# Last weight row spread by TensorE, and rewritten first steps, in the first layer of a two-layer kernel on Trainium2

## The chip, the cores and the metric

The kernel runs on one core of a Trainium2 chip. The metric is the device time of one execution in microseconds (us). TensorE is called PE here, its weight loads PEld, VectorE is DVE, ScalarE is ACT, GpSimd is POOL; SyncE (SP) issues most DMAs.

## What is computed

8192 rows of 256 go through two layers. This is the reference, cut to the first layer, the only one that the change touches:

```python
xn = _layernorm(x, axis=-1)
qkv = xn @ W;  q, k, v = jnp.split(qkv, 3, axis=-1)        # W: 256 x 768
q = elu(q) + 1;  k = elu(k) + 1
KV = einsum('bld,blh->bhd', k, v);  Z = 1 / (q . k.sum + EPS)
s = einsum('bld,bhd,bl->blh', q, KV, Z)                     # linear attention
g = silu(ffn(xn))      # the expert with the largest xn @ gate_w.T, of 8
x = x + s * g
```

The second layer has block attention, a gate with routed attention heads, and the same closing sum.

## The kernel before

All of the program is written out by hand, engine by engine; semaphores (named in `g`) tie the engines together, and what stands in an engine's function is the order in which that engine works. It has three stages: the first layer's attention with the sorting of rows by expert (to about 217 us), the experts, the second layer. The change lies in `first_layer`.

**Units and steps.** The 8192 rows are 32 units of 256 rows. Each engine has a function `step(n, i, r)` and runs it for n up to 31 in its own order. For a unit n the work goes: SP loads x into `four`; DVE takes means and variances (`norm_stats`, `find_moments`, `variance_eps`); POOL makes 1/sqrt and the shift (`norm_scale`, lines 895 and 897); ACT applies them and writes `xn` (`norm_apply`, line 529); PE transposes xn (`turn`, line 394); ACT rounds the transposed tile to fp32r and DVE takes the rest, so that a value is the sum of two fp32r numbers (`round_turned`, `split_turned`); PE makes q (`q`, 12 products of 256 columns) and k with the gate's logits (`keys`, 12 products of 264 columns); ACT takes the exponentials (`exp_q`, `exp_keys`), DVE completes them (`fill_q`, `fill_keys`), k is rounded and split (`round_keys`, `split_keys`), and PE adds k's products with xn to a sum (`sums`, 12 products). In PE's step n stand turn(n+1), q(n), keys(n) and sums(n-1). A product of two split matrices is three matmuls (`mm3`, lines 167 to 169). Every fourth unit closes a row of the batch, and `kv` multiplies the sum with the value weights; the first such product is in step 5.

**The trick with the last column.** `xn` has 1.0 in its last column in place of the last normalized value, and the last row of W is subtracted from every row of W ("centring"), since normalized rows sum to zero. The same last row is needed on all 128 partitions. Before, a DMA brings it there: `row_end`, a `partition_broadcast` of 3 KB to 128 partitions (384 KB), issued by SP behind the first part of W and ahead of the 8 KB gate weights and of the other parts. DVE's `centre_weights(part)` (lines 762 to 772) subtracts it from 256 columns of W (the parts are the weights of q, k and v) and, for q and k, adds the last column of the identity matrix to the last half, as

```python
m = nc.vector.tensor_tensor(cols, cols, row_end[...].to_broadcast([P, KD, D]), ALU.subtract)
m = nc.vector.tensor_scalar(cols[:, KD - 1, :], cols[:, KD - 1, :], z.ident[:, P - 1:P], None, ALU.add)
```

Then ACT rounds the weights (`round_weights`, line 603) and DVE takes the rest (`split_weights`, line 778): piece 0 is q's, 1 is k's, 2 is the gate's 16 columns, 3 is the values'. PE turns the gate weights with two tiny transposes (line 507) once DVE has centred them (`centre_gate`, line 760).

**The first steps.** The steps with n at most 0 differ: DVE centres parts 0 and 1 in step -2, splits pieces 0 to 2 and centres part 2 in step -1, and splits piece 3 at the start of step 1; ACT rounds pieces 0 to 2 in step -2 and piece 3 at the end of step 0.

## Time and profile before

| | |
|---|---|
| median of 3 runs | 536.98 us (535.69 to 537.85) |
| the profiled execution | 538.56 us, its span 536.9 us |
| PE busy | 503.0 us, 94% of the span |
| DVE, ACT, POOL busy | 458.7 us, 392.1 us, 315.3 us |

The span is the time between the first and the last instruction that the profiler saw. A busy PE counts matmuls whose ends are modelled, so the start-to-start distance of two matmuls says more than the duration of one. In a timeline row the bracket at the end gives how long the engine had been idle before the row, and whose work ended that.

### The profile page before, as it was taken

How to read it: one execution, taken by the hardware profiler on the slowest of the kernel's cores; microseconds unless marked ns; L12 is line 12 of the kernel's file. 1: busy time of each engine (PE TensorE's matmuls, PEld its weight loads, DVE VectorE, ACT ScalarE, POOL GpSimd, SP SyncE). 2: the span in 40 equal slices, each digit the busy share in tenths (PEclk: the TensorE clock that was granted, in tenths of full speed). 3: DMA queues.
4: the chain of work that ended last, by engine and by line, in shares of the span. 5: the costliest groups of instructions: out<-in, count | busy, mean ns of one | idle time of the engine just before them, and what ended most of it. 6: DMA issues, size and time to landing. Idle time of an engine off the chain costs nothing.

```text
span 536.9 us, 12508 instructions
## 1 busy us (share of the span) xinstructions
PE 503.0 (94%) x3554; PEld 464.4 (87%) x3555; DVE 458.7 (85%) x1475; ACT 392.1 (73%) x891; POOL 315.3 (59%) x395
## 2 busy tenths in 40 slices
PE   1899999999999999898999997899999999999995
PEld 0899999999999998787999985788888888888884
DVE  4698999999999887478787837899999999999985
ACT  3687878787878764476777744678887888779883
POOL 4458876667777876222222026868888888786410
PEclk9999999999999999899999999999999999999999
DMA  8933222222222115556677563235655656555311
GB/s 229 234 97 108 92 94 100 84 79 79 80 81 89 41 70 188 147 168 196 212 249 209 181 213 104 77 98 121 135 129 129 139 122 131 124 145 110 74 59 60
DMA packets 59552, 68.12 MB, mean 127 GB/s; under 512 B 11880, under 2 KB 53744, under 8 KB 59504
## 3 DMA queue, kind: packets, MB, share of 16 engines
q1 hardware_dynamic: 45104, 39.73, 24.4%
q0 software_dynamic: 14400, 27.80, 21.2%
q8 instruction: 24, 0.39, 0.3%
q14 instruction: 24, 0.20, 0.1%
HBM read 40.25 MB, written 27.26 MB: 126 GB/s over the span
## 4 chain that ended last, share of the span: by engine, by line
PE 59%; DVE 20%; issue 8%; POOL 6%; DMA 3%; ACT 3%; DVEq 1%; SPq 0%; POOLq 0%; ACTq 0%
PE gu_ps L1083 5%; PE v_ps L1483 4%; PE q_ps L1461 3%; PE t_ps L1059 3%; PE k_ps L167 3%; PE y_ps L1102 3%; DVE zg L1710 3%; PE k_ps L168 3%; PE tq_ps L167 3%; PE k_ps L169 3%; PE m_ps L167 3%; PE tq_ps L168 3%; PE m_ps L169 2%; PE tq_ps L169 2%; PE tq_ps L394 2%
## 5 line engine op out<-in xcount | busy, mean ns | idle before, releaser
L1830 POOL DMA_INDIRECT four<-expert_rows,gather_u x64 | 69.0, 1078 | 40.7 <-DMA expert_rows<-y 22.3
L914 POOL DMA_INDIRECT sorted_rows<-xn,row_u x64 | 68.0, 1063 | 17.2 <-issue 13.9
L903 POOL TENSOR_TENSOR xn<-xn 128x512 fp32r<-128x512 f32 x32 | 43.3, 1353 | 32.1 <-ACT xn L539 31.9
L1461 PE MATMUL q_ps<-xt,wqk 128*128 128x256 f32 x256 | 61.4, 383 | 0.8 <-ACT xt L1579 0.8
L1483 PE MATMUL v_ps<-wvo,xt 128*128 128x256 f32 x256 | 60.5, 379 | 0.0
L1461 PEld LDWEIGHTS q_ps<-xt,wqk 128*128 128x128 f32 x256 | 49.2, 193 | 7.8 <-ACT xt L1579 1.0
L205 POOL DMA_DIRECT2D four<-sorted_rows x36 | 19.4, 539 | 62.3 <-issue 32.2
L1848 POOL TENSOR_TENSOR rstd<-var_eps,neg_half 128x4 f32<-128x4 f32 x32 | 38.5, 1204 | 20.7 <-DVE var_eps L1704 11.0
L1483 PEld LDWEIGHTS v_ps<-wvo,xt 128*128 128x128 f32 x256 | 46.3, 190 | 5.0
L1599 ACT ACTIVATE xn2nd<-res,shift,rstd 128x256 f32<-128x256 f32 (+1 forms) x64 | 34.9, 594 | 19.3 <-POOL shift L1850 19.2
L1083 PE MATMUL gu_ps<-wgu,xgt 128*128 x288 | 40.2, 283 | 0.0
L529 ACT ACTIVATE xn<-four,shift,rstd 128x255 f32<-128x255 f32 x64 | 34.9, 601 | 5.9 <-POOL shift L897 5.9
L167 PE MATMUL tq_ps<-xt,wq 128*128 128x256 f32 x128 | 39.0, 305 | 0.0
L567 ACT ACTIVATE k<-kf 128x512 fp32r<-128x512 f32 x32 | 20.2, 630 | 25.0 <-DVE kf L681 25.0
L167 PE MATMUL k_ps<-wkg,xt 128*128 128x264 f32 x128 | 38.0, 297 | 0.0
L167 PE MATMUL m_ps<-k,xn 128*128 128x256 f32 x128 | 36.3, 284 | 1.2 <-DVE k L687 1.2
L168 PE MATMUL k_ps<-wkg,xt 128*128 128x264 f32 x128 | 36.8, 287 | 0.0
L169 PE MATMUL k_ps<-wkg,xt 128*128 128x264 f32 x128 | 36.6, 286 | 0.0
L1083 PEld LDWEIGHTS gu_ps<-wgu,xgt 128*128 128x128 f32 x288 | 35.0, 191 | 1.5
L168 PE MATMUL tq_ps<-xt,wq 128*128 128x256 f32 x128 | 36.3, 283 | 0.0
L169 PE MATMUL tq_ps<-xt,wq 128*128 128x256 f32 x128 | 36.2, 283 | 0.0
L169 PE MATMUL m_ps<-k,xn 128*128 128x256 f32 x128 | 36.1, 282 | 0.0
(253 smaller groups left out, 1774.2 us busy)
## 6 DMA issues: line engine op xcount, KB each, us to landing
expert_rows<-y SPq DMA_DIRECT2D x36, 256.0 KB, 2.8
four<-in_L_attn_x SPq DMA_DIRECT2D x32, 256.0 KB, 2.9
out_rows<-att SPq DMA_DIRECT2D x32, 256.0 KB, 2.5
res<-in_L_attn_x POOLq DMA_DIRECT2D x24, 256.0 KB, 4.4
four<-sorted_rows SPq DMA_DIRECT2D x36, 128.0 KB, 2.2
four<-sorted_rows POOLq DMA_DIRECT2D x36, 128.0 KB, 2.6
wdn<-in_L_ffn_wd SPq DMA_DIRECT2D x2, 512.0 KB, 7.2
sorted_rows<-res SPq DMA_DIRECT2D x8, 128.0 KB, 6.1
```

The source lines that it names most:

```text
L167: nc.tensor.matmul(out, lhs[0], rhs[0], start=first, stop=False, **kw)
L168: nc.tensor.matmul(out, lhs[0], rhs[1], start=False, stop=False, **kw)
L169: return nc.tensor.matmul(out, lhs[1], rhs[0], start=False, stop=last, **kw)
L529: m = nc.scalar.activation(xn[:, i, t, 0:D - 1], xa[:, i % X_SLOTS, t, 0:D - 1], ACT.Identity, bias=shift[:, i % X_SLOTS, t:t + 1], scale= ...
L903: nc.gpsimd.tensor_tensor(xn2[:, s, 1], xn[:, i], xn2[:, s, 0].bitcast(F32), ALU.subtract).then_inc(g["xn_split"], 1)
L914: nc.gpsimd.indirect_dma_start(out=z.sorted_dram.ap(), out_offset=bass.IndirectOffsetOnAxis(ap=row_u[:, i // CU, k:k + 1], axis=0), in_=xn ...
L1083: m = nc.tensor.matmul(gu_ps[:, i % 2, u * 2 * DE:(u + 1) * 2 * DE], xgt[:, i, k, u, :], z.wgu[:, k, bass.ds(e[u], 1), :].rearrange("p a f ...
L1461: m = nc.tensor.matmul(q_ps[:, j, :], wqk[:, k, j * P:(j + 1) * P], xt[:, i % 2, k, :], start=(j == 0 and k == 0), stop=(k == KD - 1), ski ...
L1483: m = nc.tensor.matmul(v_ps[:, t, :], xt[:, i % 2, k, t * P:(t + 1) * P], wvo[:, k, :], start=(t == 0 and k == 0), stop=(k == KD - 1), ski ...
L1599: m = nc.scalar.activation(xn[:, i % SLOTS, t, :].unsqueeze(1), one_tile(n, t), ACT.Identity, bias=shift[:, i % SLOTS, t:t + 1], scale=rst ...
L1830: nc.gpsimd.indirect_dma_start(out=moe[:, i % SLOTS, t, :], out_offset=None, in_=z.expert_dram.ap(), in_offset=bass.IndirectOffsetOnAxis(a ...
L1848: nc.gpsimd.tensor_tensor(rstd[:, i % SLOTS], var_eps[:, i % SLOTS], z.neg_half[:, 0:2 * UT].rearrange("p (a t) -> p a t", a=2), ALU.pow). ...
```

## The change

1. The broadcast DMA of the last row goes. In its place PE multiplies a 128x128 selector matrix (`last_row`, whose row 127 is all ones, made by one DVE copy of the identity's last column) with the last half of each part of W (`spread_end`): this puts the last row on all 128 partitions of a PSUM bank (`row_ends`). `centre_weights` reads it from there.
2. PE makes eight products of the identity with itself that nobody reads (`stay_warm`): six at the very start, two in step 0.
3. PE's step 0 has q(0) ahead of turn(1), and PE starts when the identity alone is there instead of all constants.
4. DVE: the split of q's weights comes right behind the centring in step -2, that of k's and the gate's behind the first split of xt in step -1, the centring of the value weights in step 0 together with `fill_q(0)` ahead of the rest, and the split of the value weights at the end of step 2.
5. ACT: in step -2 only q's weights are rounded; those of k and of the gate follow the first transposed tile; exp_q(0) comes ahead of the normalization of unit 2; the value weights are rounded ahead of `round_keys(0)`.
6. POOL makes its five casts (line 927) one step earlier, ahead of the scale of unit 1.
7. The wait and the copy of the selector stand in DVE's part a second time, at the end of the layer ahead of `table_rows`.

```diff
@@ -266,7 +266,7 @@
-        row_end = z.res[:, 4 * UT:4 * UT + 3].rearrange("p t d -> p (t d)")
+        last_row = kf[:, 1].rearrange("p t d -> p (t d)")[:, 0:P]
@@ -274,7 +274,7 @@
-        g = sems("gate_loaded moe_w_loaded ends_loaded blank consts cast gate_centred gate_turned part_centred centred rounded split step "
+        g = sems("gate_loaded moe_w_loaded selector ends_spread blank consts cast gate_centred gate_turned part_centred centred rounded split step "
@@ -321,6 +321,8 @@
         values_before = lambda n: sum(s < n for s in BESIDE_STEPS)
 
         gate_ps = v_ps[:, 0, 0:KD * E].rearrange("p (k e) -> p k e", e=E)
+        row_ends = (m_ps[:, 0, 0:D], m_ps[:, 1, 0:D], v_ps[:, 1, 0:D])
+
 
         kv_bank = lambda b: m_ps if b == UNITS // ROW - 1 else v_ps
 
@@ -352,7 +354,6 @@
                     cols = slice(part * D, (part + 1) * D)
                     sp.dma_start(w_s[:, :, cols], W[:, cols].rearrange("(k p) n -> p k n", p=P)).then_inc(w_loaded[part], 16)
                     if part == 0:
-                        sp.dma_start(row_end, W[D - 1, :].partition_broadcast(P)).then_inc(g["ends_loaded"], 16)
                         sp.dma_start(gate_s[:], gate_w).then_inc(g["gate_loaded"], 16)
 
             def step(n, i, r):
@@ -488,12 +489,26 @@
                                     [kv2[:, ORDER[p] // ROW - SPLIT_ROWS[0], a, j, :] for a in range(2)], j == 0, j == KD - 1)
                     m.then_inc(z.v_ready, 1)
 
+            def spread_end(part):
+
+                pe.wait_ge(w_loaded[part], 16)
+                nc.tensor.matmul(row_ends[part], last_row, w_s[:, KD - 1, part * D:(part + 1) * D], start=True, stop=True).then_inc(g["ends_spread"], 1)
+
+            def stay_warm(count):
+                for _ in range(count):
+                    nc.tensor.matmul(k_ps[:, 0, 0:P], z.ident[:], z.ident[:], start=True, stop=True)
+
             def step(n, i, r):
+                begin = n == 0
+                if begin:
+                    stay_warm(2)
+                    spread_end(2)
+                    pe.wait_ge(g["split"], 1)
+                    q(n, i, r)
                 turn(n + 1, at(i, 1))
-                if isinstance(n, int) and n == 0:
-                    pe.wait_ge(g["split"], 1)
-                q(n, i, r)
-                if isinstance(n, int) and n == 0:
+                if not begin:
+                    q(n, i, r)
+                if begin:
                     pe.wait_ge(g["split"], 3)
                     pe.wait_ge(g["cast"], 5)
                 keys(n, i, r)
@@ -501,11 +516,15 @@
                 sums(n - 1, at(i, -1), r if i else r - 1)
                 values(n)
 
-            pe.wait_ge(g["consts"], 6)
+            pe.wait_ge(g["consts"], 1)
+            stay_warm(6)
+            pe.wait_ge(g["selector"], 1)
+            spread_end(0)
             pe.wait_ge(g["gate_centred"], 1)
             for k in range(KD):
                 t = nc.tensor.transpose(gate_ps[:, k], gate_c[:, k * P:(k + 1) * P], z.ident[0:E, 0:E])
             t.then_inc(g["gate_turned"], 1)
+            spread_end(1)
             run(pe, -1, step, UNITS - 1)
             whole_values(nc, pe, z, TAIL[0], tail_banks(TAIL[0]), SPLIT)
             count(UNITS, 0, 0)
@@ -608,21 +627,26 @@
                 round_sums(n, i, r)
                 if begin and n == -2:
                     norm_apply(0, 0)
-                    round_weights((0, 1, 2))
+                    round_weights((0,))
                 round_turned(n + 1, at(i, 1))
+                if begin:
+                    exp_q(n, i)
+                if begin and n == -1:
+                    round_weights((1, 2))
                 if begin and n > -2:
                     norm_apply(n + 2, at(i, 2))
                 round_xn(n, i)
                 rows(value_of(n - 1))
-                exp_q(n, i)
+                if not begin:
+                    exp_q(n, i)
                 if not begin:
                     norm_apply(n + 2, at(i, 2))
                 exp_keys(n, i)
                 round_kv(n, i, r)
                 round_next(value_of(n + 1))
-                round_keys(n, i)
                 if begin and n == 0:
                     round_weights((3,))
+                round_keys(n, i)
 
             run(act, -2, step, UNITS - 1)
             rows(TAIL[0])
@@ -761,12 +785,10 @@
 
             def centre_weights(part):
                 cols = w_s[:, :, part * D:(part + 1) * D]
-                dve.wait_ge(w_loaded[part], 16)
-                dve.wait_ge(g["ends_loaded"], 16)
-                m = nc.vector.tensor_tensor(cols, cols, row_end[:, part * D:(part + 1) * D].unsqueeze(1).to_broadcast([P, KD, D]), ALU.subtract)
+                dve.wait_ge(g["ends_spread"], part + 1)
+                m = nc.vector.tensor_tensor(cols, cols, row_ends[part].unsqueeze(1).to_broadcast([P, KD, D]), ALU.subtract)
                 if part < 2:
                     m.then_inc(g["part_centred"], 1)
-                    dve.wait_ge(g["consts"], 6)
                     dve.wait_ge(g["part_centred"], part + 1)
                     m = nc.vector.tensor_scalar(cols[:, KD - 1, :], cols[:, KD - 1, :], z.ident[:, P - 1:P], None, ALU.add)
                 m.then_inc(g["centred"], 1)
@@ -846,33 +868,39 @@
                     centre_gate()
                     centre_weights(0)
                     centre_weights(1)
-                if begin and n == -1:
-                    split_weights((0, 1, 2))
+                    split_weights((0,))
+                if begin and n == 0:
                     centre_weights(2)
-                if begin and n == 1:
-                    sum_columns()
-                    split_weights((3,))
+                    fill_q(n, i)
                 split_keys(n - 1, at(i, -1))
                 split_kv(n - 1)
                 divisors(value_of(n - 1))
                 if there(n):
                     split_sums(n, i, r)
                 split_turned(n + 1, at(i, 1))
+                if begin and n == -1:
+                    split_weights((1, 2))
                 split_next(value_of(n))
                 norm_stats(*ahead)
                 stats_complete(*ahead)
-                fill_q(n, i)
+                if not (begin and n == 0):
+                    fill_q(n, i)
                 find_moments(*ahead)
                 negate_mean(*ahead)
                 variance_eps(*ahead)
                 fill_keys(n, i)
                 route_and_place(n, i, r)
                 keep_pick(n, i, r)
+                if n == 2:
+                    sum_columns()
+                    split_weights((3,))
                 if isinstance(n, int) and n >= UNITS - 8 and n % CU == 0:
                     centre_experts((n - UNITS + 8) // CU)
 
             nc.vector.memset(one_col[:], 1.0)
             nc.vector.memset(change[:, E - 1:E], 0.0)
+            dve.wait_ge(g["consts"], 1)
+            nc.vector.tensor_copy(last_row, z.ident[:, P - 1:P].to_broadcast([P, P])).then_inc(g["selector"], 1)
             run(dve, -3, step, UNITS - 1)
             split_keys(UNITS - 1, SLOTS - 1)
             divisors(TAIL[0])
@@ -882,6 +910,8 @@
             table_owners()
             table_offsets()
             divisors(TAIL[1])
+            dve.wait_ge(g["consts"], 1)
+            nc.vector.tensor_copy(last_row, z.ident[:, P - 1:P].to_broadcast([P, P])).then_inc(g["selector"], 1)
             table_rows()
             divisors(TAIL[2])
             table_names()
@@ -921,7 +951,7 @@
 
             def step(n, i, r):
                 norm_scale(n + 2, at(i, 2))
-                if isinstance(n, int) and n == -1:
+                if isinstance(n, int) and n == -2:
                     for dst, src in ((z.ones_b, ones_s), (z.before, tri_s), (z.causal, causal_s),
                                      (z.ident_b, z.ident[:]), (z.slot_id, ids[:])):
                         nc.gpsimd.tensor_copy(dst[:], src).then_inc(g["cast"], 1)
```

PE's first instructions before (`tq_ps` holds the transposed tile and q, `v_ps<-ident,gate_c` are the gate's transposes):

```order
L507 MATMUL v_ps<-ident,gate_c 128x8 [waits first_gate_centred,first_consts]
L507 MATMUL v_ps<-ident,gate_c 128x8
L394 MATMUL tq_ps<-ident,xn 128x128 [waits first_xn_ready]
L394 MATMUL tq_ps<-ident,xn 128x128 x3
L394 MATMUL tq_ps<-ident,xn 128x128 [waits first_t_split,first_xn_ready]
L394 MATMUL tq_ps<-ident,xn 128x128 x3
L167 MATMUL tq_ps<-xt,wq 128x256 [waits first_t_split,first_split]
```

and after the change (`k_ps<-ident` are the unread products, `<-w_s,kf` the spreading of the last row):

```order
L499 MATMUL k_ps<-ident 128x128 [waits first_consts]
L499 MATMUL k_ps<-ident 128x128 x5
L495 MATMUL m_ps<-w_s,kf 128x256 [waits w_loaded0,first_selector]
L525 MATMUL v_ps<-ident,gate_c 128x8 [waits first_gate_centred]
L525 MATMUL v_ps<-ident,gate_c 128x8
L495 MATMUL m_ps<-w_s,kf 128x256 [waits w_loaded1]
L395 MATMUL tq_ps<-ident,xn 128x128 [waits first_xn_ready]
L395 MATMUL tq_ps<-ident,xn 128x128 x3
L499 MATMUL k_ps<-ident 128x128 x2
L495 MATMUL v_ps<-w_s,kf 128x256 [waits w_loaded2]
L167 MATMUL tq_ps<-xt,wq 128x256 [waits first_t_split,first_split]
```

Eight unread products and three spreading products are new, and q(0), the row with `tq_ps<-xt,wq`, now stands ahead of the second group of transposes.

DVE from the end of the centring to the value weights' centring, before (`w_s` is W, `wq` and `wkg` the split weights, `xt` the transposed tile):

```order
L640 BN_STATS stats<-four 128x6 [waits x_loaded1]
L640 BN_STATS stats<-four 128x6
L652 BN_AGGR moments<-stats 128x2 [waits first_stats_done]
L652 BN_AGGR moments<-stats 128x2
L658 TENSOR_SCALAR neg_mean<-moments 128x2 [waits first_moments_ready]
L663 TENSOR_SCALAR var_eps<-moments 128x2
L778 TENSOR_TENSOR wq<-w_s,wq 128x512 [waits first_rounded]
L778 TENSOR_TENSOR wkg<-w_s,wkg 128x2x256 [waits first_rounded]
L778 TENSOR_TENSOR wkg<-v_ps,wkg 128x2x8 [waits first_rounded]
L766 TENSOR_TENSOR w_s<-w_s,res 128x2x256 [waits first_ends_loaded,w_loaded2]
L668 TENSOR_TENSOR xt<-tq_ps,xt 128x512 [waits first_t_rounded]
```

and after:

```order
L800 TENSOR_TENSOR wq<-w_s,wq 128x512 [waits first_rounded]
L664 BN_STATS stats<-four 128x6 [waits x_loaded1]
L664 BN_STATS stats<-four 128x6
L676 BN_AGGR moments<-stats 128x2 [waits first_stats_done]
L676 BN_AGGR moments<-stats 128x2
L682 TENSOR_SCALAR neg_mean<-moments 128x2 [waits first_moments_ready]
L687 TENSOR_SCALAR var_eps<-moments 128x2
L692 TENSOR_TENSOR xt<-tq_ps,xt 128x512 [waits first_t_rounded]
L800 TENSOR_TENSOR wkg<-w_s,wkg 128x2x256 [waits first_rounded]
L800 TENSOR_TENSOR wkg<-v_ps,wkg 128x2x8 [waits first_rounded]
```

The split of `wq` has moved ahead of the statistics of unit 1, the first split of `xt` stands right behind them, and the splits of `wkg` and the centring of the value weights come later.

ACT behind its first normalization, before (`kf` and `k` belong to the keys, `res` to q):

```order
L603 ACTIVATE wq<-w_s 128x512 [waits first_centred]
L603 ACTIVATE wkg<-w_s 128x2x256 [waits first_centred]
L603 ACTIVATE wkg<-v_ps 128x2x8 [waits first_gate_turned]
L544 ACTIVATE xt<-tq_ps 128x512 [waits first_t_ready]
L529 ACTIVATE xn<-four,shift,rstd 128x255 [waits first_shift_ready]
L529 ACTIVATE xn<-four,shift,rstd 128x255
L544 ACTIVATE xt<-tq_ps 128x512 [waits first_t_ready]
L529 ACTIVATE xn<-four,shift,rstd 128x255 [waits first_shift_ready]
L529 ACTIVATE xn<-four,shift,rstd 128x255
L539 ACTIVATE xn<-xn 128x512 [waits first_xn_ready]
L552 ACTIVATE res<-tq_ps,minus_one 128x512 [waits first_q_ready]
L560 ACTIVATE kf<-k_ps,minus_one 128x512 [waits first_k_ready]
```

and after:

```order
L622 ACTIVATE wq<-w_s 128x512 [waits first_centred]
L563 ACTIVATE xt<-tq_ps 128x512 [waits first_t_ready]
L622 ACTIVATE wkg<-w_s 128x2x256 [waits first_centred]
L622 ACTIVATE wkg<-v_ps 128x2x8 [waits first_gate_turned]
L548 ACTIVATE xn<-four,shift,rstd 128x255 [waits first_shift_ready]
L548 ACTIVATE xn<-four,shift,rstd 128x255
L563 ACTIVATE xt<-tq_ps 128x512 [waits first_t_ready]
L571 ACTIVATE res<-tq_ps,minus_one 128x512 [waits first_q_ready]
L548 ACTIVATE xn<-four,shift,rstd 128x255 [waits first_shift_ready]
L548 ACTIVATE xn<-four,shift,rstd 128x255
L558 ACTIVATE xn<-xn 128x512 [waits first_xn_ready]
L579 ACTIVATE kf<-k_ps,minus_one 128x512 [waits first_k_ready]
```

The first `xt` is one copy earlier, `res` (exp_q(0)) is ahead of unit 2's normalization, and the last row is k's exponential in both.

## Rows read from the trace of the kernel before

**Rows 1.** The page, busy time of each engine: us, share of the span, instructions.

```profile
PE 503.0 (94%) x3554; PEld 464.4 (87%) x3555; DVE 458.7 (85%) x1475; ACT 392.1 (73%) x891; POOL 315.3 (59%) x395
```

**Rows 2.** Windows: stretch, length, busy of PE, PEld, DVE, ACT, POOL, PEclk, DMA.

```profile
40.00:60.00 20.00, 20.00 (x177) 19.90 (x177) 18.09 (x69) 16.14 (x30) 17.68 (x21) 1.00 0.33 107
...
180.00:200.00 20.00, 20.00 (x178) 19.90 (x177) 17.30 (x60) 14.59 (x29) 15.81 (x16) 1.00 0.16 61
```

**Rows 3.** Timeline of PE: start, duration, engine, line, operation, count, idle before.

```profile
14.63 1.11 PE L394 MATMUL tq_ps<-ident,xn 128*128 128x128 f32 x4 [4.91 <-ACT xn L529]
...
15.76 0.41 PE L168 MATMUL tq_ps<-xt,wq 128*128 128x256 f32 x1
...
18.10 0.42 PE L167 MATMUL k_ps<-wkg,xt 128*128 128x264 f32 x1
...
19.64 0.36 PE L168 MATMUL k_ps<-wkg,xt 128*128 128x264 f32 x1
...
20.32 0.60 PE L394 MATMUL tq_ps<-ident,xn 128*128 128x128 f32 x4
...
24.60 0.36 PE L167 MATMUL m_ps<-k,xn 128*128 128x256 f32 x1 [0.80 <-DVE k L687]
...
26.11 0.60 PE L394 MATMUL tq_ps<-ident,xn 128*128 128x128 f32 x4
```

**Rows 4.** Windows of PE alone: stretch, length, busy, granted clock, DMA share, GB/s.

```profile
15.74:19.80 4.06, 4.06 (x21) 1.00 1.11 210
```

**Rows 5.** Timeline of SP, issues of the first two weight parts.

```profile
1.44 0.46 SPq L353 DMA_DIRECT2D w_s<-in_L_attn_W  x1
...
2.88 0.39 SPq L353 DMA_DIRECT2D w_s<-in_L_attn_W  x1
```

**Rows 6.** DMA issues in 1.4 to 1.9 and in 2.85 to 3.3: us to landing.

```profile
w_s<-in_L_attn_W SPq DMA_DIRECT2D x1, 256.0 KB, 2.9
w_s<-in_L_attn_W SPq DMA_DIRECT2D x1, 256.0 KB, 5.8
```

**Rows 7.** Timeline of DVE in the first 25 us.

```profile
7.84 0.34 DVE L760 TENSOR_SCALAR gate_c<-gate_s 8x256 f32<-8x256 f32 x1 [2.83 <-DMA gate_s<-in_L_ffn_gate_w]
8.11 0.67 DVE L766 TENSOR_TENSOR w_s<-w_s,res 128x512 f32<-128x512 f32 x1
...
10.22 0.74 DVE L640 BATCH_NORM_STATS2 stats<-four 128x6 f32<-128x256 f32 x2
...
11.36 0.16 DVE L663 TENSOR_SCALAR var_eps<-moments 128x2 f32<-128x2 f32 x1
...
13.32 0.68 DVE L668 TENSOR_TENSOR xt<-tq_ps,xt 128x512 fp32r<-128x512 f32 x1
...
23.16 0.69 DVE L778 TENSOR_TENSOR wv<-w_s,wv 128x512 fp32r<-128x512 f32 x1 [0.92 <-ACT wv L603]
23.76 0.69 DVE L687 TENSOR_TENSOR k<-kf,k 128x512 fp32r<-128x512 f32 x1
```

**Rows 8.** Timeline of ACT in the first 23 us.

```profile
6.20 1.09 ACT L529 ACTIVATE xn<-four,shift,rstd 128x255 f32<-128x255 f32 x2 [3.97 <-POOL shift L897]
...
15.78 0.60 ACT L544 ACTIVATE xt<-tq_ps 128x512 fp32r<-128x512 f32 x1 [1.20 <-PE tq_ps L394]
...
20.53 0.69 ACT L560 ACTIVATE kf<-k_ps,minus_one 128x512 f32<-128x512 f32 x1 [1.50 <-PE k_ps L169]
21.97 0.63 ACT L567 ACTIVATE k<-kf 128x512 fp32r<-128x512 f32 x1 [0.75 <-DVE kf L681]
```

**Rows 9.** Timeline of POOL, two of its reciprocal square roots.

```profile
11.60 1.07 POOL L895 TENSOR_TENSOR rstd<-var_eps,neg_half 128x2 f32<-128x2 f32 x1 [5.44 <-DVE var_eps L663]
...
15.30 0.71 POOL L895 TENSOR_TENSOR rstd<-var_eps,neg_half 128x2 f32<-128x2 f32 x1 [0.72 <-DVE var_eps L663]
```

**Rows 10.** Timelines of DVE and of SP at the end of the layer.

```profile
214.56 0.20 DVE L835 CAST row_i<-first_row 128x72 int32<-128x72 f32 x1
...
216.81 5.47 SPq L205 DMA_DIRECT2D four<-sorted_rows  x5
```

## The prediction, made before the changed kernel ran

> **What bounds the kernel now.** I read the page first: PE is busy for 94% of the span [rows 1]. The windows then show where it is not. From 40 to 60 us and from 180 to 200 us PE is busy for all 20.00 us while DVE has 1.9 to 2.7 us left [rows 2]; the six windows of 20 us between these two also have PE at 20.00. So once the layer runs, PE is the bound, its work is fixed, and whatever the start saves is kept. The timeline of PE shows the start: it waits 4.91 us until 14.63, when unit 1 is normalized, waits another 0.80 us at 24.60 for DVE's split of k, and reaches turn(3) at 26.11 [rows 3]. Behind that it has no idle time worth a row until 200 us. **The time of turn(3) is therefore the quantity to predict.** Before, it is 26.11.
>
> PE also runs at half rate at first. The granted clock reads 1.00 from 15.74 to 19.80 [rows 4], but the 11 products from 15.76 to 18.10 are (18.10 - 15.76)/11 = 0.213 us apart, which is 256 columns at 1.2 GHz; at 19.64 the durations begin to fall from 0.42, and the 12 products from 24.60 to 26.11 are 0.126 us apart, the 2.4 GHz level [rows 3]. PE had worked without a pause from 14.63 before it rose.
>
> **Where the start waits.** The first part of W is issued at 1.44 and lands 2.9 us later, at 4.34; the second is issued at 2.88 and needs 5.8, to 8.68 [rows 5, 6]. Between them in the queue stand only the broadcast of 384 KB and the gate's 8 KB. DVE is idle for 2.83 us until the gate weights land at 7.84, and from there it works without a gap: centring from 8.11, statistics of unit 1 from 10.22 to 11.52, first split of xt at 13.32 [rows 7]. POOL and ACT add 1.07 us and more, and that makes the 14.63 of PE [rows 3, 9].
>
> **The change, part by part.**
>
> *Loads.* Without the broadcast the gate and the second part are issued one place earlier, near 2.0 and 2.4. Bounds for the second part's landing: 2.4 + 2.9 = 5.3 if it takes what the first did, 2.4 + 5.8 = 8.2 if the broadcast was not what delayed it. I take 5.3, since the first part had no broadcast ahead of it and is the nearest row.
>
> *Selector and unread products.* The DVE copy of 128x128 falls into DVE's idle time ahead of 3.7 us, before x has come: 0. If that cover were gone it would cost at most the 0.69 us of a 512-wide operation [rows 7]. The six unread products run between about 2 and 4.6 us, when PE has nothing else. An fp32 product of 256 columns at half rate has no row here. Its bounds are the 0.41 us that a rounded one lasts and twice that, 0.82 [rows 3]; I take the upper one for it, because it must not be late: 4.34 + 0.82 = 5.2.
>
> *Centring.* DVE is free at 7.84 - 2.83 = 5.01. The gate takes 8.11 - 7.84 = 0.27, so part 0 is centred from about 5.4, by which time its spread row is there, and part 1 follows; both took 10.22 - 8.11 = 2.11 [rows 7], so 7.5. The operand is now in PSUM: the split of xt, which reads PSUM, takes 0.68 us, the centring out of SBUF 0.67 [rows 7], so I add nothing. The Trainium skill (VectorE: DVE Perf Modes, the TRN2 errata) speaks against this edit, since it gives an operation on PSUM a fixed cost of 120 cycles instead of 58; that would be about 0.07 us each, 0.14 us for the two centrings on the path; the rows do not show it.
>
> *Up to q(0).* ACT normalizes unit 0 from 6.20 for 1.09 us [rows 8], then rounds q's weights until 7.9. DVE splits them (0.60 to the next start, 23.76 - 23.16) until 8.5, does the statistics of unit 1 (1.2, from 10.22 to just behind the start at 11.36) until 9.7 and splits xt until 10.4 [rows 7]. PE turns unit 0 at 7.4, ACT has it rounded by 7.4 + 1.15 + 0.60 = 9.2 [rows 3, 8], so it is not late. q(0) starts at 10.4.
>
> *PE's first block.* turn(1), q(0) and keys(0) took 20.32 - 14.63 = 5.69 at mostly half rate [rows 3]. In the new order and at the same rate they end at 16.1, turn(1) starting at 10.4 + 12 x 0.213 = 13.0. It needs unit 1: its variance is ready at 9.8, and from POOL's start at 11.60 to PE's at 14.63, over POOL and ACT, 3.0 us passed [rows 3, 9], so 12.8. It is 0.2 in time. The two fillers and the spreading of part 2 stand in the wait ahead of 10.4.
>
> *ACT.* Its copy of unit 1's tile follows 15.78 - 14.63 = 1.15 after the turn [rows 3, 8], at 14.15. Behind it stand that copy, exp_q(0), two normalizations and one rounding, about 0.55 + 0.55 + 1.0 + 0.55 = 2.65 by the starts of such rows, so k's exponential begins at 16.8, not at 20.53 [rows 8]: 3.7 earlier.
>
> *From there to turn(3).* Before, 20.53 to 21.97 (exponential, completion), then the rounding, DVE's split of the value weights at 23.16 and only then that of k at 23.76, sums(0) at 24.60 [rows 3, 7, 8]. After, DVE comes to k's completion about 0.3 late, since fill_q(0), the split of xt and the statistics stand ahead; rounding at 16.8 + 1.44 + 0.3 = 18.5, split of k over by 19.9, for the 0.60 of the value weights no longer stands there. PE meanwhile does turn(2) and q(1), waits to 18.6 for keys(1), and ends it at 20.1; sums(0) takes 26.11 - 24.60 = 1.5, to 21.6 [rows 3]. Unit 3 is normalized at 21.7. **turn(3) stands at 21.8, so the gain is 26.11 - 21.8 = 4.3 us.**
>
> *What is late next.* The split of the value weights and sum_columns are put at the end of step 2, 0.60 + 0.25 on DVE. The step before it carried the routing, this one does not, and kv comes only in step 5: 0. The gate's and k's splits behind xt are done by 11.5, keys(0) asks at 13.8: 0. POOL's casts run beside DVE's centring: 0. At the layer's end the second copy of the selector costs DVE up to 0.7, but the table is written at 214.56 + 0.20 and SP issues the loads that need it at 216.81 [rows 10]: 0, with 2.0 us of cover.
>
> **Sum.** The profiled execution took 538.56 us, so it becomes 534.3. That execution lay 1.6 above the median of 536.98, and against the median I predict 536.98 - 4.3 = **532.7 us**. The three runs lie 2.2 apart, so about 0.5% (2.7 us) is what a measurement can tell from no change.
>
> **Rivals.**
>
> *Full rate earlier (0.25).* PE now works from 7.4 to about 9.4 and again from 10.4, instead of pausing for 4.91 us. If that lets the clock rise by 13.0, then turn(1) and keys(0) take half, some 1.6 us less, of which ACT's chain lets through 0.7: gain 5.0, 532.0 us. For it: PE's pause of 4.91 us ahead of the half-rate stretch [rows 3]. Against it: PE rose only after 5 us of unbroken work then. The Trainium skill (TensorE: Matmul & The Clock Gate, Part 1 and Part 4) says that activity releases the throttle at a moment that varies from run to run, and that transposes do not count as activity as products do; by that the unread products would bring this case about, and no row here separates the two.
>
> *The lag moves to DVE (0.10).* DVE has 1.9 us left in 20 [rows 2] and is 0.3 later against PE than before. If every early step then costs PE 0.5 for four steps, the gain is 2.3: 534.7 us. Against it: sums(1) still comes after the routing in my schedule.
>
> *The broadcast was not the delay (0.10).* If the gate still lands near 7.8, then centring starts as before and only the order helps: q(0) follows its own chain, 2.4 us later than above. Gain 1.9: 535.1 us. For it: landing times of 5.8 us at full queues [rows 6]. Against it: nothing else stood between the two landings.
>
> *Slower (0.05).* The half rate outlasts the new pauses. PE now stops near 13.0, 16.1 and 18.6, and if the clock only rises after unbroken work as from 14.63, it stays at 1.2 GHz, and each full step of 36 products costs 36 x (0.213 - 0.126) = 3.1 us more than at 2.4. It decides from 1.4 such steps on, where the 4.3 is used up; with 2.5 steps more at half rate the result is +3.5 us, 540.5.
>
> **How the numbers follow.** Forecast 0.50, the rivals 0.25, 0.10, 0.10 and 0.05. Faster by over 0.5% is the forecast and the first rival, 0.75; within 0.5% are the next two, 0.20; slower 0.05. The range starts at the first rival's 532.0 less 1.6 for the scatter of medians and a clock that rises earlier still, 530.4, and ends at the third rival's 535.1 plus 0.7 of scatter, 535.8; the slower case and the outer edges are left out. The forecast's own range is 531.2 to 534.2.
>
> **What would show it.** Gate weights centred near 5.0 instead of 7.84; q's first product near 10.4 and ahead of turn(1); k's exponential near 16.8; no wait of sums(0) for the value weights; turn(3) near 21.8; PE full from there; distances of 0.213 us until about 16. I am wrong if DVE still waits until 7.8 for a load, if turn(3) is early but PE shows idle time between 22 and 60 us, or if distances of 0.21 us go on behind 20 us.

## The result and the profile after

The changed kernel took **534.06 us** (median of 20 runs, 532.03 to 537.18), the one before 536.62 in the same comparison (20 runs). Two of those 20, at 577.24 and 642.45 us, stand far apart and are not in the ratio; the other 18 have a median of 536.26. The ratio is **0.9954, with an interval of 0.9938 to 0.9970**: faster by 2.5 us, between 1.6 and 3.3. The forecast was 532.7 us, from a gain of 4.3. The time lies in the range, and the gain is 1.8 us short: by its middle, 0.46%, it is just within the 0.5% that had been given 0.20, and not in the class above it that had 0.75; the interval reaches to 0.62%.

The profiled execution took 533.15 us, with a span of 531.5, against 538.56 and 536.9 before. That pair alone would say 5.4 us. Why the pair says 5.4 and the medians 2.5 is one of the two questions of this part; the other is which piece of the change made the gain. A part of the first is in the windows of the kernel before, columns as in [rows 2]:

```profile
218.00:224.00 6.00, 4.14 (x17) 3.16 (x16) 2.26 (x6) 2.88 (x6) 2.64 (x6) 0.77 0.70 221
```

The granted clock is 0.77 there and 1.00 in the same stretch of the changed kernel, and 6.0 x 0.23 = 1.4 us is an estimate of what that cost. With the 3.9 us of the start, below, it makes up 5.3 of the 5.4. The 1.4 belongs to this one execution and not to the change: a second profile of the kernel before reads 1.00 there. PE's work barely grew, by the rows of the eight unread products and the three that spread the row, two rows each [rows 1]:

```profile
PE 504.9 (95%) x3576; PEld 463.8 (87%) x3577; DVE 460.0 (87%) x1477; ACT 391.6 (74%) x891; POOL 315.7 (59%) x395
```

The windows of the changed kernel, columns as in [rows 2]. From 20 us on PE is busy for all of each stretch of 20 us, as far as 200:

```profile
12.00:15.00 3.00, 3.00 (x16) 3.00 (x15) 1.31 (x6) 1.49 (x4) 0.89 (x2) 0.50 1.27 223
20.00:40.00 20.00, 20.00 (x174) 19.55 (x173) 18.84 (x69) 15.96 (x31) 12.49 (x13) 1.00 0.50 158
180.00:200.00 20.00, 20.00 (x177) 19.90 (x176) 15.73 (x48) 14.35 (x27) 16.17 (x16) 1.00 0.17 66
```

The first row is of another kind. The granted clock reads 0.50 there, so PE was at 1.2 GHz from 12 to 15 us, *after* it had been at 2.4. The timeline of PE shows the same, and answers to [rows 3]:

```profile
4.73 0.73 PE L495 MATMUL m_ps<-w_s,kf 128*128 128x256 f32 x2
...
6.67 0.70 PE L495 MATMUL m_ps<-w_s,kf 128*128 128x256 f32 x2 [0.93 <-DMA w_s<-in_L_attn_W]
...
11.04 0.35 PE L167 MATMUL tq_ps<-xt,wq 128*128 128x256 f32 x1 [2.03 <-DVE xt L692]
...
11.35 0.28 PE L169 MATMUL tq_ps<-xt,wq 128*128 128x256 f32 x1
11.46 0.28 PE L167 MATMUL tq_ps<-xt,wq 128*128 128x256 f32 x1
...
12.02 0.41 PE L168 MATMUL tq_ps<-xt,wq 128*128 128x256 f32 x1
12.24 0.41 PE L169 MATMUL tq_ps<-xt,wq 128*128 128x256 f32 x1
...
13.09 1.05 PE L395 MATMUL tq_ps<-ident,xn 128*128 128x128 f32 x4
...
16.82 0.63 PE L395 MATMUL tq_ps<-ident,xn 128*128 128x128 f32 x4 [0.68 <-DVE xt L692]
...
19.04 0.39 PE L167 MATMUL k_ps<-wkg,xt 128*128 128x264 f32 x1 [0.18 <-DVE logit L706]
...
20.60 0.28 PE L167 MATMUL m_ps<-k,xn 128*128 128x256 f32 x1
...
22.18 0.65 PE L395 MATMUL tq_ps<-ident,xn 128*128 128x128 f32 x4
```

q(0) starts at 11.04 and its products are 0.12 us apart up to 11.82, then 0.21 apart until 15.04. turn(1) comes behind q(0), at 13.09, with no wait. keys(0) ends just before 16, turn(2) waits 0.68 us for DVE's split of xt, keys(1) waits 0.18, and sums(0) does not wait at all, where it waited 0.80 before [rows 3]. **turn(3) stands at 22.18 instead of 26.11: 3.93 us earlier.** The span less the time of turn(3) is 510.8 us before and 509.3 after, so in this pair the gain at the start is kept to the end.

DVE, answering to [rows 7]:

```profile
5.06 0.33 DVE L784 TENSOR_SCALAR gate_c<-gate_s 8x256 f32<-8x256 f32 x1
5.49 0.69 DVE L789 TENSOR_TENSOR w_s<-w_s,m_ps 128x512 f32<-128x512 f32 x1
...
7.40 0.69 DVE L789 TENSOR_TENSOR w_s<-w_s,m_ps 128x512 f32<-128x512 f32 x1 [0.73 <-PE m_ps L495]
...
8.40 0.68 DVE L800 TENSOR_TENSOR wq<-w_s,wq 128x512 fp32r<-128x512 f32 x1
...
15.39 0.69 DVE L699 SCALAR_TENSOR_TENSOR res<-res,tq_ps 128x512 f32<-128x512 f32 x1 [2.01 <-ACT res L571]
...
17.65 0.59 DVE L682 TENSOR_SCALAR neg_mean<-moments 128x2 f32<-128x2 f32 x1
...
18.22 0.68 DVE L705 SCALAR_TENSOR_TENSOR kf<-kf,k_ps 128x512 f32<-128x512 f32 x1
...
19.59 0.69 DVE L711 TENSOR_TENSOR k<-kf,k 128x512 fp32r<-128x512 f32 x1 [0.61 <-ACT k L586]
...
28.64 0.69 DVE L800 TENSOR_TENSOR wv<-w_s,wv 128x512 fp32r<-128x512 f32 x1
```

The gate weights are centred at 5.06 without a wait, where DVE had been idle for 2.83 us until 7.84. At 7.40 stands the one wait of DVE ahead of q(0) that the forecast did not have, 0.73 us for the spread row of part 1, which itself waited 0.93 us for that part (PE, 6.67). The load of part 1 and its us to landing, answering to [rows 5, 6]:

```profile
2.40 0.38 SPq L355 DMA_DIRECT2D w_s<-in_L_attn_W  x1
```

```profile
w_s<-in_L_attn_W SPq DMA_DIRECT2D x1, 256.0 KB, 4.2
```

And ACT, answering to [rows 8]:

```profile
16.75 0.68 ACT L579 ACTIVATE kf<-k_ps,minus_one 128x512 f32<-128x512 f32 x1
...
18.93 0.63 ACT L586 ACTIVATE k<-kf 128x512 fp32r<-128x512 f32 x1 [0.98 <-DVE kf L705]
```

### The profile page after: what moved, and what is told of

Read it like the earlier page. It is cut to its first block, busy times and chain, and to the rows that moved or that the text cites. A ratio compares the mean times of both kernels' runs of the same rounds, so it can differ in the third digit from the quotient of the medians.

```text
span 531.5 us, 12547 instructions
## 1 busy us (share of the span) xinstructions
PE 504.9 (95%) x3576; PEld 463.8 (87%) x3577; DVE 460.0 (87%) x1477; ACT 391.6 (74%) x891; POOL 315.7 (59%) x395
## 3 DMA queue, kind: packets, MB, share of 16 engines
q1 hardware_dynamic: 44960, 39.34, 24.3%
## 4 chain that ended last, share of the span: by engine, by line
PE 61%; DVE 21%; issue 7%; DMA 4%; POOL 3%; ACT 2%; DVEq 1%; SPq 1%; POOLq 0%; ACTq 0%
PE gu_ps L1113 5%; PE v_ps L1513 4%; PE q_ps L1491 3%; PE k_ps L167 3%; PE m_ps L167 3%; PE m_ps L169 3%; PE t_ps L1089 3%; PE m_ps L168 3%; PE tq_ps L167 3%; PE k_ps L168 3%; PE k_ps L169 3%; PE y_ps L1132 3%; PE tq_ps L168 3%; PE tq_ps L169 3%; DVE zg L1740 3%
## 5 line engine op out<-in xcount | busy, mean ns | idle before, releaser
L167 PE MATMUL tq_ps<-xt,wq 128*128 128x256 f32 x128 | 38.6, 302 | 2.0 <-DVE xt L692 2.0
L167 PE MATMUL m_ps<-k,xn 128*128 128x256 f32 x128 | 36.2, 283 | 0.4 <-DVE k L711 0.4
L169 PE MATMUL m_ps<-k,xn 128*128 128x256 f32 x128 | 36.1, 282 | 0.0
L168 PE MATMUL m_ps<-k,xn 128*128 128x256 f32 x128 | 36.1, 282 | 0.0
L168 PE MATMUL tq_ps<-xt,wq 128*128 128x256 f32 x128 | 36.0, 281 | 0.0
```

Of the source, the lines that this page charges most:

```text
L167: nc.tensor.matmul(out, lhs[0], rhs[0], start=first, stop=False, **kw)
L168: nc.tensor.matmul(out, lhs[0], rhs[1], start=False, stop=False, **kw)
L169: return nc.tensor.matmul(out, lhs[1], rhs[0], start=False, stop=last, **kw)
```

## The experiments

"Changed kernel again" and "kernel before again" are the same two programs on other chips. Within one comparison the kernels ran on one chip; the ratios are to the kernel before there. A kernel with one execution only, its profiled one, has no ratio.

| kernel | ratio to before | turn(3) in its profile |
|---|---|---|
| kernel before again | none | 25.56 |
| only the spread row | 0.9977 (0.9954 to 1.0001) | 24.71 |
| only the order | 1.0001 (0.9974 to 1.0027) | 24.34 |
| changed, no unread products | 0.9965 (0.9943 to 0.9987) | 23.22 |
| changed kernel again | 0.9953 (0.9930 to 0.9975) | 21.52 |
| changed, more unread products | 0.9933 (0.9910 to 0.9957) | 22.43 |
| changed, part 1 by ACT's queue | 0.9961 (0.9940 to 0.9982) | 21.53 |
| changed, value split early | none | 22.74 |
| changed, turn(1) ahead of q(0) | 0.9974 (0.9950 to 0.9997) | 24.30 |
| changed, keys sooner | 0.9948 (0.9926 to 0.9971) | 21.49 |
| keys sooner, waits filled | 0.9901 (0.9871 to 0.9932) | 21.57 |
| changed, wait at the layer's end filled | 0.9947 (0.9926 to 0.9969) | 21.06 |

**The kernel before, again.** No edit.

> The kernel before, looked at a second time. My theory: the two profiled executions lie 5.4 us apart in span and only 3.9 apart at turn(3), and the rest is TensorE's clock, which stands at half rate in other stretches in each execution. Then this look shows turn(3) within 1.5 us of 26.11, but not at it, with the distances of 0.213 us ending at another time than 19.8, and the eight transposes at the layer's end (1.71 us before) may take another time. The rival, that turn(3) does not depend on the clock's phase: 26.1 within 0.2 again.

Measured: 537.26 us, span 535.6. The timeline of PE:

```profile
14.81 1.11 PE L394 MATMUL tq_ps<-ident,xn 128*128 128x128 f32 x4 [4.91 <-ACT xn L529]
...
24.05 0.36 PE L167 MATMUL m_ps<-k,xn 128*128 128x256 f32 x1 [0.80 <-DVE k L687]
...
25.56 0.60 PE L394 MATMUL tq_ps<-ident,xn 128*128 128x128 f32 x4
```

The same program starts its first block 0.18 us later than in [rows 3] and is at turn(3) 0.55 us sooner, because the spacing fell from 0.21 to 0.12 us at 18.3 instead of 19.8. So turn(3) of one profiled execution is good to some 0.5 us, by the moment at which the clock rises.

**Only the spread row.** The loads without the broadcast, the selector and the products that spread the row, in the order of before:

```diff
-                        sp.dma_start(row_end, W[D - 1, :].partition_broadcast(P)).then_inc(g["ends_loaded"], 16)
+                nc.tensor.matmul(row_ends[part], last_row, w_s[:, KD - 1, part * D:(part + 1) * D], start=True, stop=True).then_inc(g["ends_spread"], 1)
```

> Only the broadcast is replaced by the spreading products; all orders stay as before, and there are no unread products. If the loads were what mattered, most of the gain is here: centring of part 0 near 5.6 instead of 8.11, turn(1) near 12.5, turn(3) near 24.2, ratio about 0.9965. If the order of the steps is what mattered, turn(3) stays at 25.5 or later and the ratio above 0.998.

```profile
13.15 1.10 PE L394 MATMUL tq_ps<-ident,xn 128*128 128x128 f32 x4 [3.31 <-ACT xn L539]
...
23.20 0.36 PE L167 MATMUL m_ps<-k,xn 128*128 128x256 f32 x1 [0.80 <-DVE k L697]
```

Unit 1 is normalized 1.5 us sooner (13.15 for 14.63), but the block of turn(1), q(0) and keys(0) still takes 5.78 us at half rate, and the wait of 0.80 us for k is still there. The loads did what was expected of them (part 0 centred at 5.84 for 5.6, turn(1) at 13.15 for 12.5), and turn(3), at 24.71, and the ratio of 0.9977 lie between the two cases; the interval of the ratio holds both 0.9965 and no gain.

**Only the order.** The broadcast stays; the steps, the splits and the unread products are those of the changed kernel:

```diff
-                turn(n + 1, at(i, 1))
+                begin = n == 0
+                if begin:
+                    stay_warm(2)
...
+                    q(n, i, r)
+                turn(n + 1, at(i, 1))
```

> The changed kernel with the broadcast DMA back in its old place and no spreading products; the new order of the steps and the unread products stay. If the loads mattered: gate weights land at 7.8 again, q(0) starts near 13.3, turn(3) near 24.3 (1.8 us gained by the order alone, as the third rival of the prediction had it), ratio about 0.997. If the two parts only work together, turn(3) stays near 26.

```profile
12.55 0.55 PE L167 MATMUL tq_ps<-xt,wq 128*128 128x256 f32 x1 [2.20 <-DVE xt L684]
...
15.25 1.05 PE L396 MATMUL tq_ps<-ident,xn 128*128 128x128 f32 x4
```

q(0) starts 2.1 us before PE's first turn of the kernel before, turn(3) is 1.2 to 1.8 us sooner than in its two profiles, as was expected (24.34 for 24.3), and yet the ratio is 1.0001 where 0.997 was: what turn(3) gained did not come out in the median, and why stays open. By their middles neither half gives the whole, 0.23% and 0.00% against 0.46%, but the interval of the first, 0.9954 to 1.0001, reaches to the ratio of the changed kernel, and that was measured on another chip. turn(3) is clearer: 0.9 to 1.4 us sooner by the spread row, 1.2 to 1.8 by the order, 3.4 to 4.6 by both. (Seven of the 12 executions of this kernel had a low mean clock; the section on the clock has more.)

**Turn(1) ahead of q(0).** The changed kernel with this one pair in its old order:

```diff
-                    pe.wait_ge(g["split"], 1)
-                    q(n, i, r)
                 turn(n + 1, at(i, 1))
-                if not begin:
-                    q(n, i, r)
+                if begin:
+                    pe.wait_ge(g["split"], 1)
+                q(n, i, r)
```

> Undoes one part of the changed kernel: in TensorE's step 0 the turn of xn(1) stands ahead of q(0) again. Theory (the lag is set by VectorE's and ScalarE's work on the tiles, and a turn that waits for xn(1) holds q(0) back by some 1 us): q(0) begins after turn(1), near 13.2 instead of 11.0 to 11.2, keys(0) near 14.0 as in the changed kernel or up to 0.6 later, and turn(3) between 21.8 and 22.6, where the changed kernel showed 22.18 and 21.52. Ratio to the kernel before 0.995 to 0.997. Rival (the order on TensorE is what the change gains by): turn(3) over 23.0 and a ratio of 0.998 or more.

```profile
13.07 1.12 PE L395 MATMUL tq_ps<-ident,xn 128*128 128x128 f32 x4 [2.79 <-ACT xn L547]
...
18.94 0.63 PE L395 MATMUL tq_ps<-ident,xn 128*128 128x128 f32 x4 [0.17 <-DVE xt L691]
```

The theory gave too little for this piece. turn(3), at 24.30, lies beyond the 23.0 that the rival asked for; the ratio of 0.9974 lies between the theory's 0.997 and the rival's 0.998, where "only the spread row" stands. The first row shows the mechanism: PE waits 2.79 us for ACT's xn(1), and turn(1), q(0) and keys(0) fill 5.87 us after it, nearly all at half rate (the spacing fell only at 17.9). In the changed kernel the same block begins at 11.04 and fills 5.78 to turn(2). So **moving q(0) into the wait for unit 1 is worth 2.1 us at turn(2)** in this pair of profiles. Some of that is the clock: against "no unread products", which has the new order and q(0) at half rate as well, it is 1.1 us (turn(2) at 17.88), with q(0) there 0.6 us late for its weights. The move needs the spread row, since without that q(0) has its operands 1.5 us later.

**No unread products.** Both calls of `stay_warm` go.

> The changed kernel without its eight unread products. They raised the clock before q(0) (distances of 0.12 us from 11.04 to 11.8), but it fell back before turn(1). My theory: without them q(0) runs at half rate throughout and ends at 13.3 instead of 13.1, and keys(0) may stay at half rate longer; turn(3) 22.2 to 22.8, ratio to the kernel before 0.995 to 0.997, that is no more than 0.5 us worse than the changed kernel. The rival, that the unread products carry the gain: turn(3) later than 23.5 and a ratio of 0.998 or more.

```profile
6.74 1.22 PE L495 MATMUL m_ps<-w_s,kf 128*128 128x256 f32 x2 [0.61 <-DMA w_s<-in_L_attn_W]
```

Measured 0.9965, where the theory had it, beside 0.9954 and 0.9953 with them: the intervals overlap, so time tells nothing apart. The profile does. The pair of rows that spreads part 1's row lasts 1.22 us here, 0.70 in the changed kernel (PE, 6.67), q(0) starts at 11.63 and runs at half rate until 15.15, and turn(3) is at 23.22, 1.0 to 1.7 us later than in the two profiles of the changed kernel: later than the theory's 22.2 to 22.8 and sooner than the rival's 23.5. Some 0.6 us of it stands ahead of q(0), where part 1's row comes later and DVE waits 1.06 us for it.

All profiles together: **with six unread products at 2.0 us, q(0) started at full rate in 8 of 10 profiles** (not in "only the order" and "turn(1) ahead of q(0)"), and in 5 of the 9 that spread the row by products, the pair of part 1 already lasted 0.70. **Without them, q(0) ran at half rate in all 4** (both profiles of before, "only the spread row", this one). Only this last one differs from the changed kernel in nothing else, so the count leans on one profile. What the early rise gives is partly taken back: in 3 of those 5 PE fell back to half rate during the first block, as in the changed kernel at 11.82.

**More unread products.** Three groups of two more between PE's early turns, gated so that they fall into the wait ahead of q(0):

```diff
+                    pe.wait_ge(g["rounded"], 1)
+                    stay_warm(2)
+                    pe.wait_ge(g["rounded"], 3)
+                    stay_warm(2)
+                    pe.wait_ge(g["stats_done"], 2 * UT)
+                    stay_warm(2)
```

> The changed kernel with eight more unread products in TensorE's wait ahead of q(0), in four pairs, each behind an event of that wait, the last behind the statistics of unit 1. They fill the 2.03 us between 9.0 and 11.04. My theory, that idle time ahead of q(0) let the clock fall back: products 0.12 us apart from q(0) through keys(0), turn(1) at 12.7 when unit 1 is normalized instead of 13.09, turn(3) at 21.4 to 21.6, 0.6 to 0.8 earlier than in the changed kernel. The rival, that TensorE's rate in step 0 is hidden behind ScalarE: turn(3) at 22.0 or later. The last pair may delay q(0) by up to 0.3 at half rate.

```profile
7.13 1.22 PE L495 MATMUL m_ps<-w_s,kf 128*128 128x256 f32 x2 [1.02 <-DMA w_s<-in_L_attn_W]
```

Two things at once. In this execution PE was still at half rate before 10.7 (the spread pair of part 1 lasts 1.22 us instead of 0.70), and part 1 landed 0.5 us later, so q(0) began at 12.30. From there PE was at full rate, and turn(3) followed 10.13 us behind q(0), against 11.14 in the first profile of the changed kernel and 10.37 in the second. turn(3) itself, at 22.43, missed the theory's 21.4 to 21.6 and lies where the rival had it, but by the late landing of part 1 and not because PE's rate is hidden. Ratio 0.9933: the middle is 0.2% better than the changed kernel's, the interval does not part them.

**The changed kernel again.** No edit.

> The changed kernel itself, looked at again, with the others of this call as neighbours. The clock rose early and fell back at 11.8 in its first look. If that is the chance of one execution, the half-rate stretch lies elsewhere now and turn(3) is between 21.6 and 22.8; the ratio to the kernel before is 0.995 within 0.002.

```profile
11.15 0.36 PE L167 MATMUL tq_ps<-xt,wq 128*128 128x256 f32 x1 [0.91 <-DVE xt L692]
...
16.18 0.63 PE L395 MATMUL tq_ps<-ident,xn 128*128 128x128 f32 x4 [1.19 <-DVE xt L692]
...
21.52 0.66 PE L395 MATMUL tq_ps<-ident,xn 128*128 128x128 f32 x4
```

Here the clock rose later, during the wait ahead of q(0) (the pair of part 1 at 6.26 still lasted 1.22 us), and held: the spacing is 0.12 us from 11.15 on. q(0) and turn(1) are over sooner, turn(2) therefore *waits longer* for DVE, 1.19 us for 0.68, and of the 1.6 us that the half rate had cost PE (half of 11.82 to 15.04) only 0.66 show at turn(3). Part 1 landed sooner here too, 3.8 us after its issue for 4.2; over the profiles without the broadcast it took from 3.8 to 4.7.

**Part 1 of the weights by ACT's queue.**

```diff
-                    load_weights((0, 1) if m == 0 else (2,))
+                    load_weights((0,) if m == 0 else (2,))
...
+            act.dma_start(w_s[:, :, D:2 * D], W[:, D:2 * D].rearrange("(k p) n -> p k n", p=P)).then_inc(w_loaded[1], 16)
```

> The changed kernel with the second part of W issued by ScalarE's DMA queue at its very start instead of third but one on SyncE's. In the changed kernel it landed at 6.6 and DVE waited 0.73 us for its spread row at 7.40. If the place in the queue is the delay, it lands by 5.3, the wait goes, q(0) starts at 10.3 and turn(3) 0.6 to 0.7 earlier, at 21.5. If the memory's rate is the delay, the first part or x land later by as much and turn(3) stays within 0.2 of 22.2.

```profile
w_s<-in_L_attn_W ACTq DMA_DIRECT2D x1, 256.0 KB, 3.6
w_s<-in_L_attn_W SPq DMA_DIRECT2D x1, 256.0 KB, 3.8
```

```profile
4.33 0.75 DVE L665 BATCH_NORM_STATS2 stats<-four 128x6 f32<-128x256 f32 x2 [2.03 <-DMA four<-in_L_attn_x]
...
6.54 0.69 DVE L790 TENSOR_TENSOR w_s<-w_s,m_ps 128x512 f32<-128x512 f32 x1 [0.67 <-PE m_ps L495]
```

Part 1 is issued 1.45 us sooner and lands at 0.95 + 3.6 = 4.55 instead of 6.6. But part 0 now takes 3.8 us instead of 3.0, and the first tile's statistics start at 4.33 instead of 3.85. DVE waits 0.67 us for part 0's row instead of 0.73 for part 1's, and q(0) starts at 11.17. **What one load gains the others lose**: in this profile another queue made no gain ahead of q(0), so the place in the queue was not the delay. turn(3) at 21.53 is what the first theory had named, but by luck: PE was at full rate from q(0) on, as in the second profile of the changed kernel, whose turn(3) stands at 21.52.

**The value weights split early**, where they stood before:

```diff
+                if begin and n == 1:
+                    sum_columns()
+                    split_weights((3,))
```

> The changed kernel with the rounding of the value weights behind that of k, and their split at the start of step 1, as before the change. DVE then waits for ScalarE and splits them ahead of k: 0.60 and the three small operations, 0.8 to 1.4 us before k's split. turn(3) 23.0 to 23.6. The rival, that ScalarE's normalization of unit 3 sets turn(3) anyway: 22.4 or earlier.

```profile
21.23 0.36 PE L167 MATMUL m_ps<-k,xn 128*128 128x256 f32 x1 [0.80 <-DVE k L711]
```

The wait of 0.80 us for k is back, to the hundredth what it was in [rows 3]. turn(3) is at 22.74, though q(0) began at 11.01, between the theory's 23.0 and the rival's 22.4. The new place is worth 0.6 us at turn(3) against the first profile of the changed kernel, in which the clock fell back as it did here, and costs nothing at step 2, where PE has no idle row.

**Keys sooner.** An attempt at a better kernel. DVE's step 0 takes the centring of part 2, the split of xt(1) and the keys' bias ahead of the next moments, ACT takes k's exponential ahead of the rounding of xn(0) and rounds the value weights a step later, and the selector is not copied again:

```diff
+                    split_turned(n + 1, at(i, 1))
...
+                    norm_stats(*ahead)
+                    stats_complete(*ahead)
+                    fill_keys(n, i)
...
+                if begin:
+                    exp_keys(n, i)
```

> Adds to the changed kernel: VectorE's step 0 takes the centring of part 2, the split of xt(1), the keys' bias and only then the moments of the next tiles, ScalarE takes the keys' exponential of step 0 ahead of the rounding of xn(0), the value weights are rounded a step later, and the second copy of the selector goes. Theory (after the first projection the lag is the work on VectorE and ScalarE in order, not TensorE): turn(2) near 15.8 and turn(3) at 20.5 to 20.9, against 16.18 and 21.52, and a ratio near 0.9935. Rival (by then TensorE at its granted clock or the keys' chain elsewhere sets the lag): turn(3) at 21.3 or later and a ratio of 0.995 as in the changed kernel.

```profile
10.96 0.36 PE L167 MATMUL tq_ps<-xt,wq 128*128 128x256 f32 x1 [1.92 <-DVE xt L694]
...
12.64 1.11 PE L395 MATMUL tq_ps<-ident,xn 128*128 128x128 f32 x4
```

```profile
17.02 0.69 DVE L707 SCALAR_TENSOR_TENSOR kf<-kf,k_ps 128x512 f32<-128x512 f32 x1 [0.64 <-ACT kf L579]
...
17.98 0.85 DVE L684 TENSOR_SCALAR neg_mean<-moments 128x2 f32<-128x2 f32 x1
```

k's completion came forward, to 17.02 from 17.57 in the second profile of the changed kernel. But the moments of unit 3 now stand behind it (17.98, and that row is stretched to 0.85 us), so unit 3 is normalized no sooner, and turn(3) waits 0.21 us for it, at 21.49. By its numbers the rival is right, and the ratio of 0.9948 is that of the changed kernel. But this execution is not like the one it is set beside: PE fell back to half rate at turn(1) (the four transposes at 12.64 last 1.11 us, not 0.66) and stayed there until 15.8. **Counted from q(0) and at the same clock the new order does gain**: turn(3) follows 10.53 us behind q(0) here, where the changed kernel with such a fall took 11.14; at full rate throughout, the next experiment has 9.69 us, and four profiles of the order of the changed kernel have 10.13 to 10.37. That is 0.4 to 0.7 us of the 1.0 that the theory had, and too little for the ratio to show.

This execution also had half rate after the layer's end, as that of before had (0.77 in the window 218 to 224). Windows:

```profile
217.00:224.00 7.00, 5.87 (x21) 5.12 (x21) 0.33 (x2) 2.03 (x4) 1.07 (x2) 0.51 0.40 121
```

The wait ahead of it is PE's for the first sorted rows, here 2.29 us, 1.86 in the profile of before, 1.72 in that of the changed kernel, where nothing fell. The length of the wait does not decide it: the second profile of before waited 2.37 us and "only the order" 2.54, and neither fell.

**Waits filled.** The kernel with the keys sooner, five gated unread products ahead of q(0), and 7 identity products in that wait at the layer's end:

```diff
+                if isinstance(n, int) and n == 0:
+                    pe.wait_ge(z.kv_split, len(SPLIT_ROWS) + len(WHOLE_ROWS))
+                    for _ in range(7):
+                        nc.tensor.matmul(t_ps[:, 0, 0, 0, :], z.ident[:], z.ident[:], start=True, stop=True)
```

> The kernel with the keys sooner, and besides 5 gated groups of the identity products ahead of q(0) and 7 identity products in the wait of TensorE for the first sorted rows at the layer's end; nothing reads what they make. Theory (part of the spread between executions is TensorE's granted clock, which falls after such a wait): no stretch of half rate after the layer's end, turn(3) at 20.5 to 20.9, and a ratio of 0.992 to 0.993. Rival (the stretch of half rate comes and goes whatever stands in the wait, or it is covered by other waits): a ratio equal to that of the kernel with the keys sooner.

```profile
217.00:224.00 7.00, 6.57 (x44) 6.11 (x45) 1.37 (x6) 3.12 (x8) 1.61 (x3) 1.00 0.48 153
331.00:336.00 5.00, 5.00 (x18) 4.06 (x18) 4.83 (x16) 2.46 (x5) 4.42 (x6) 0.66 0.21 62
```

533.15 us, where the kernel without the filling ran 535.79 on the same chip in the same comparison, and **the ratio is the best of all, 0.9901 (0.9871 to 0.9932)**. Its 6 executions lie within 1.0 us, below 10 of the 12 of the kernel without it, which spread over 4.3. The gain is not at turn(3), which stands at 21.57 for 21.49 and not at the theory's 20.5 to 20.9, since q(0) began only at 11.88. It lies behind it, where the span less turn(3) is 510.5 us for 513.5. After the layer's end the clock is at 1.00, PE busy 6.57 us of 7 instead of 5.87. A stretch of half rate still stands near 331 to 334. Of the 12 profiles without products in that wait, five have half rate somewhere from 217 to 225 us; of the two with them, none. Two are too few to tell this from chance, so the rival, that the stretch comes and goes, is not ruled out.

**Only the layer's end filled.** The changed kernel with the last diff alone.

> The changed kernel as it is, with 7 identity products that nothing reads in TensorE's wait for the first sorted rows at the layer's end; its first steps are untouched. Theory (of the 2.6 us by which the kernel with both sorts of filling ran below the one with the keys sooner, most is the layer's end: the wait there lets the granted clock fall in some executions, and a stretch at half rate of 3.4 us costs up to 1.7 us): no half rate within 20 us after the layer's end, ratio 0.990 to 0.992, and a spread of the executions under 3 us where the changed kernel showed 5. Rival (it was the filling ahead of the first projection): a half-rate stretch still shows after the layer's end or nothing changes, ratio 0.994 to 0.996.

```profile
213.42 1.72 PE L1083 MATMUL t_ps<-ident 128*128 128x128 f32 x14
214.98 0.62 PE L1093 MATMUL t_ps<-ident,four 128*128 128x128 f32 x4
```

The products are where they should be, the rows after them run at full rate, and no half rate shows within 20 us (there is one later, a clock of 0.66 from 340 to 345), but the time did not follow: 0.9947, the spread 4.1 us, and three of 11 executions above 535. By time the theory's 0.990 to 0.992 is missed. So the layer's end alone does not show the gain of the kernel with both fillings, and turn(3) does not show that of the products ahead of q(0). Which of them it is, or both together, was not tried apart on one chip, and the two intervals overlap (0.9926 to 0.9932), so this stays open.

## Executions at the same clock

The record has the mean granted clock of each execution. Sorted by it, the 97 executions of the kernel before for which it is recorded (four comparisons, each on a chip of its own) and all 32 of the changed kernel (two comparisons) give:

| mean granted clock | before: share, median us | changed: share, median us | difference |
|---|---|---|---|
| 0.998 and above | 36 of 97, 536.75 | 11 of 32, 533.07 | 3.7 |
| 0.994 to 0.997 | 46 of 97, 538.16 | 11 of 32, 534.58 | 3.6 |
| 0.993 and below | 15 of 97, 539.80 | 10 of 32, 535.93 | 3.9 |

**At equal mean clock the change gives 3.6 to 3.9 us**, near the 3.9 that turn(3) shows. Three things weaken this. The chips are not the same ones on both sides: the median of before's top row alone goes from 536.09 to 537.12 from chip to chip, and on the one chip that has both kernels the three differences are 4.2, 3.0 and 4.9 us, from 3 to 6 executions of the changed one each. (The second profiles of the two kernels, at mean clocks of 0.998 and 0.999, lie 4.4 us apart, of which 4.0 at turn(3).) The sorting was made after the times were known. And the clock is not recorded alike: the half rate at the start of the kernel before reads as 1.00 [rows 4], while the fall at 12 us in the changed kernel is recorded, and 3.2 us at half rate are some 0.003 of the mean, a whole row of this table.

The changed kernel has 31% of its executions in the lowest row, the one before 15%; the rows are about 3 us apart from top to bottom, so by these shares that is an estimate of 0.3 us of the mean. Some of that surplus may be the record of the start only. "Turn(1) ahead of q(0)" and "only the order" have 7 of 12 there, but so has the kernel with more unread products, whose start has the fewest pauses, while "only the spread row" has 2 of 12 and "waits filled" 1 of 6. What brings an execution into the lowest row is not shown.

## Why the prediction was right or wrong

**The bound, right.** PE had 20.00 of 20 before, and has them after, so what turn(3) gains is kept as far as 200 us: span less turn(3) is 509.3 and 509.7 in the two profiles of the changed kernel, 510.8 and 510.1 in those of the one before. Nor did the lag move to DVE, as the second rival had it: PE has no idle time behind turn(3) up to there. But behind 200 us the executions differ: over the other ten profiles span less turn(3) goes from 509.5 to 513.5, which is as much as the whole gain.

**The broadcast as the delay, right.** The gate is centred at 5.06 (forecast 5.0), part 0 at 5.49 (5.4). The spread product of part 0, a pair of rows, took 0.73 us at 4.73. The bound of 0.82 was none, though: at half rate the pair takes 1.0 to 1.2 us, as in the second profile (4.73 to 5.72), where DVE waits 0.48 us for it; in the first it was in time because the clock had risen.

**Part 1's landing, wrong by 1.3 us.** The step that took 2.9 us from issue to landing, "since the first part had no broadcast ahead of it", failed: it took 4.2, to 6.6, inside the bounds 5.3 to 8.2. Not only the broadcast had stood around this load but also the tiles of x, and that a load which goes sooner makes them and the other part later is what the experiment with ACT's queue shows. Of the 1.3 us the centring passed on 0.9 (both parts over at 8.4, not 7.5); ACT's rounding of q's weights, over at 7.9 as forecast, hid 0.4 of that, and with 0.1 more in the split of xt q(0) came at 11.04 instead of 10.4.

**Centring from PSUM, right.** The row at 7.40 lasts 0.69 us and the next operation starts 0.73 after it; out of SBUF before they lasted 0.67 to 0.69. By the fixed cost that the Trainium skill gives (VectorE: DVE Perf Modes, TRN2 errata) the forecast had named 0.07 us for each; the rows allow at most 0.02.

**PE's first block, right in its end, not in its way.** turn(1) at 13.09 (13.0), keys(0) over at 16.0 (16.1): q(0) started 0.6 late and won 0.5 of that back by its first six products at full rate. ACT's copy of the tile at 14.18 (14.15) and k's exponential at 16.75 (16.8) follow.

**DVE behind k's exponential, mis-sized.** "About 0.3 late" was 0.8: DVE's rows behind 15.39 run up to k's completion at 18.22, with a moments row of 0.59 us (17.65) that lasts 0.17 where nothing stretches it. Rounding at 18.93 for 18.5, keys(1) at 19.04 for 18.6, turn(3) at 22.18 for 21.8. This is the 0.4 us between the forecast gain of 4.3 and the 3.93 of the profile. The stretched row ends when a row of POOL ends; changed kernel first, then the kernel before, whose row at 20.02 lasts 0.17:

```profile
16.93 1.29 POOL L933 TENSOR_TENSOR xn<-xn 128x512 fp32r<-128x512 f32 x1 [3.09 <-ACT xn L558]
...
18.01 1.28 POOL L903 TENSOR_TENSOR xn<-xn 128x512 fp32r<-128x512 f32 x1 [1.72 <-ACT xn L539]
```

POOL's split of xn(0) is over at 18.22, DVE's row at 18.24; before, POOL was done at 19.29, ahead of DVE's row. In all eleven profiles with the new order of DVE and ACT this row lasts 0.57 to 0.85 us and ends within 0.05 us of POOL's, and in the three with the old order it lasts 0.17. So the new order brings the two rows together, and that is the term the forecast had at nothing. That POOL's row holds DVE's is argued from this coincidence; no run moved it.

**The first rival, seen.** In the second profile of the changed kernel the full rate held from q(0) on, turn(3) was at 21.52, and of PE's 1.6 us 0.66 came through; the rival had said 0.7. So both happen, from execution to execution of one program. The Trainium skill says that activity releases the throttle at a moment that varies from run to run (TensorE: Matmul & The Clock Gate, Part 1), and the two profiles agree as to the moment (at 4.7 us in one, between 9 and 11 in the other). As to the activity the count of profiles above agrees, 8 of 10 with the unread products and none of 4 without, of which one is like the changed kernel in all else. Of the three profiles with exactly these first steps (the two and "wait at the layer's end filled") the full rate held in two, so the chance of 0.25 was too low for this case.

**From turn(3) to the median, the step that failed.** The forecast took the median of before less the gain at turn(3), as if the clock later in the program were the same. Its rival of a clock that stays low named the first 25 us only. In fact each kernel's executions spread over some 4 to 5 us, with stretches at half rate later on in some, and the changed kernel's stood in the lowest row of the table more often. That accounts for 0.3 us at most of the missing 1.8, and the term on DVE for 0.4. The 1.1 us that are left are more than the interval of the ratio gives (0.85 us to either side), and their cause stays open; turn(3) of both kernels is known from two executions each, and the four differences between them go from 3.4 to 4.6 us. The base helped the forecast, by luck: 536.98 was the median of three, and the 18 executions in the ratio have 536.26. From that base the same gain would have given 532.0, which is 2.1 us under the measured time instead of 1.4.

**Costs put at nothing, right.** The value split stands at 28.64 with PE idle nowhere near it. The second copy of the selector takes 0.21 us at the layer's end; the table is written by 210.87 and SP issues the loads that need it at 212.15, so 1.3 us of cover are left of the forecast's 2.0. The splits of the gate and of k ended at 11.6, and keys(0) asked at 13.8.

## What to carry to other kernels

Moving a product that has its operands into the wait of one that has not was worth about as much at turn(3) as removing the load that made both wait (1.2 to 1.8 us and 0.9 to 1.4), and in the measured time either alone could not be told from nothing; try such edits together before one is dropped. Judge a start-up edit at the first point behind which the bound engine never idles, but do not expect that gain in the medians while the executions of one kernel spread by more than it. Before an edit is called worth nothing by one profile, see that the clock did the same in both: the order with the keys sooner seemed to gain nothing until it was counted from q(0) between profiles of like clock.

## What was not expected of the hardware

- PE's clock can be up before the first real product and fall again in it. In the changed kernel the spread pairs at 4.73 and 6.67 ran at 2.4 GHz, q(0) from 11.04 to 11.82 too, behind an idle time of 2.03 us, and then 1.2 GHz until 15.04. In the second profile it rose during the wait of 0.91 us ahead of q(0) and stayed.
- The granted clock in the windows reads 1.00 before its first recorded rise or fall even where the spacing of products is 0.21 us [rows 3, 4]; in the profile after it reads 0.50 from 12 to 15 us for the same spacing. At a program's start only the spacing tells.
- An fp32 product of 256 columns stands in the trace as two rows, together 0.60 to 0.73 us at 2.4 GHz and 1.06 to 1.22 at 1.2.
- Two executions of one program differ by up to 5 us with PE's work the same: the changed kernel's lay between 532.03 and 537.18 in the first comparison, the longer ones mostly those of a lower granted clock.
- Seven identity products in a wait of 1.7 to 2.3 us for a DMA cost nothing that the profile shows: the first four turns follow them at 214.98, where the changed kernel, which enters the wait 1.1 us later, began at 216.41, and the next four, at 216.18, still wait 0.58 us for the DMA.
- A DVE row of two elements, 0.17 us long, can last 0.57 to 0.85 us when it starts beside a long row of POOL, and then ends with that row, to 0.05 us.
